# Two graph attention layers: row scores with turned probabilities replaced by transposed scores in column chunks

## The chip, the cores and the metric

The kernel runs on one core of one Trainium2 chip. The metric is the device time in microseconds (us) of one execution. The kernel before takes 551.01 us (median of 3 runs, 550.63 to 551.37).

## The reference

Four graph layers on `x` (1354 x 256, f32) with one adjacency matrix `adj` (1354 x 1354, f32, sparse, with a weighted diagonal), each followed by a residual addition and a layer norm. The change touches only the fourth, which is two attention layers in a row. Cut to what matters:

```python
def _gat_layer(x, W, adj):                # W: 256 x 512
    proj = x @ W
    Wh, Ws = jnp.split(proj, 2, axis=-1)
    scores = Wh @ Ws.T                    # 1354 x 1354
    a = jax.nn.softmax(scores, axis=-1) * adj
    out = a @ Wh
    out = out + x
    return jax.nn.leaky_relu(out, 0.01)
# L3: x = inputs; for l in range(2): x = _gat_layer(x, W_stack[l], adj)
x = _layernorm(x + _L3_gnn_ref(x, adj, L3_gnn_W_stack), axis=-1)
```

## The kernel before

The 1354 rows are T = 11 tiles of P = 128 rows (the last has 74); the 256 features are KD = 2 blocks of 128. The 1354 columns are three chunks `CH` of 512, 512 and 330, one PSUM bank of 512 f32 each. `adjT` holds the whole transposed adjacency in SBUF, `x_all` the features by rows. Each engine has one hand-written instruction stream, in the order of its block (`block.sync`, `gpsimd`, `scalar`, `vector`, `tensor`); streams meet at semaphores only. So an instruction that waits holds up everything that stands behind it on its engine.

The first three layers and their norms end with a loop over tiles in which TensorE makes the third layer's output (`c_proj`), turns the normed rows (`turn_mean`), and makes `Wh` of the first attention layer (`wh_mean`). The score matrix is computed as x (Wh-weights Ws-weights^T) x^T, with the 256 x 256 product `M3` made once.

Each attention layer then goes over the 11 row tiles, through `pipeline`, which repeats stages with fixed lags:

- TensorE: `q` (x of this tile times `M3`, 4 matmuls of 128 columns), `turn_probs` (11 transposes of 128 x 128 of the tile before), the scores of a whole row tile (`scores.__call__`, 6 matmuls into banks 0 to 2), and `agg_d` (11 matmuls of 256 columns into bank 6). In the first layer also `turn_x` and `proj_d` for the next layer's features.
- VectorE: `row_max` (one reduction over 1354 columns in PSUM), `turn_evac` (turned probabilities times `adjT`, 1408 columns from PSUM), and the finish of a tile (`gat_out`, `finish_d1` or `finish_d2`, `norm_apply_d`).
- ScalarE: `q_evac`, and `exp_row`, one exponential over 1354 columns straight from PSUM with the row's maximum as bias, which gives the row's sum as well.
- GpSimd: `store_x` in the first layer, `rsqrt_d` in the second: one small instruction a tile.

The lines that the argument names: L1278 scores, L1311 turned probabilities, L1325 sum over neighbours, L1254 q, L1240 `proj_d`, L1203 `wh_mean`, L915 row maximum, L908 and L905 evacuation with the product, L648 exponential. From an earlier stage, as prices: L771 and L773 (VectorE on two SBUF inputs of 1354 columns), L412 (GpSimd addition of 1354 columns), L838 (VectorE on PSUM and SBUF).

## Time and profile before

| | |
|---|---|
| median of 3 runs | 551.01 us (550.63 to 551.37) |
| the profiled execution's own time | 551.62 us |
| its span, first to last instruction | 549.8 us |
| TensorE busy | 503.4 us (92%), mean granted clock 0.984 |
| VectorE, ScalarE, GpSimd busy | 308.0, 197.2, 101.2 us |
| attention layers, first `q` to last sum on TensorE | 271.9 to 542.6 us |

The page gives for each engine its busy time, then 40 equal slices of the span with busy tenths, then the chain of work that ended last. The lines of an instruction group give its count, its busy time and the mean length of one. The timeline gives single instructions with start, length, and the idle time in front with what ended it.

### The profile page before, as it was taken

Reading aid. Unit: us, or ns where it says so; the run is one execution under the profiler, and the core shown is the slowest. Engines: PE = TensorE matmul, PEld = TensorE weight load, DVE = VectorE, ACT = ScalarE, POOL = GpSimd, SP = SyncE. Lnnn points to the kernel's source line nnn. Section 1 sums busy time; section 2 is a strip of 40 time slices with the busy share of each in tenths; the row PEclk is TensorE's granted clock in tenths of the full one; section 3 lists DMA queues with packets and bytes.
Section 4 is the critical chain, followed back from the end, with each engine's and each line's share of the span. In section 5 each row is a group of like instructions: output and inputs, shape, how many; then the busy total and the mean of one; then the engine's idle time right before and its main releaser. Section 6 shows DMA issues by size and latency. Waiting matters only on the chain.

```text
span 549.8 us, 6538 instructions
## 1 busy us (share of the span) xinstructions
PE 503.4 (92%) x2321; PEld 369.7 (67%) x2321; DVE 308.0 (56%) x632; ACT 197.2 (36%) x341; POOL 101.2 (18%) x120
## 2 busy tenths in 40 slices
PE   2689999999999779799889999999998999999994
PEld 1579955555555567678557777777785777767773
DVE  2489978945999758756233333333323354455544
ACT  3347729983785522243312222222222112111120
POOL 5002152602235235633000000000000000000000
PEclk9999999999999869999999999999999999999998
DMA  8445420000652000000000000000000000000000
GB/s 252 172 146 160 119 103 0 0 0 1 196 168 72 0 0 1 0 1 1 1 0 1 0 1 0 0 0 0 0 1 1 0 17 12 10 10 10 19 10 15
DMA packets 8109, 20.60 MB, mean 37 GB/s; under 512 B 944, under 2 KB 4676, under 8 KB 8088
## 3 DMA queue, kind: packets, MB, share of 16 engines
q1 hardware_dynamic: 6808, 18.75, 10.5%
q0 software_dynamic: 464, 0.79, 0.6%
q10 hardware_dynamic: 816, 0.79, 0.4%
q8 instruction: 12, 0.20, 0.2%
q14 instruction: 9, 0.07, 0.0%
HBM read 18.94 MB, written 1.39 MB: 37 GB/s over the span
## 4 chain that ended last, share of the span: by engine, by line
PE 54%; issue 26%; DVE 13%; DMA 3%; POOL 2%; ACT 2%; SPq 0%; POOLq 0%; DVEq 0%; ACTq 0%
PE psum L1325 10%; PE psum L1278 9%; PE psum L1049 9%; PE psum L1025 4%; PE psum L1136 4%; DVE eb L771 4%; DMA x_all<-in_x_dram 3%; PE psum L1311 2%; PE psum L1254 2%; PE psum L1203 2%; PE psum L981 2%; PE psum L1162 2%; PE psum L1074 2%; PE psum L1240 1%; DVE maskT L787 1%
## 5 line engine op out<-in xcount | busy, mean ns | idle before, releaser
L1325 PE MATMUL psum<-feats,probsT 128*128 128x256 f32 (+1 forms) x484 | 108.2, 379 | 0.9 <-DVE probsT L905 0.9
L1278 PE MATMUL psum<-xT,Qs 128*128 128x512 f32 (+1 forms) x264 | 104.1, 543 | 1.2 <-ACT xTs L612 0.7
L1325 PEld LDWEIGHTS psum<-feats,probsT 128*128 128x128 f32 (+1 forms) x484 | 91.6, 190 | 15.3 <-issue 1.1
L908 DVE TENSOR_TENSOR probsT<-psum,adjT 128x1408 f32<-128x1408 f32 x20 | 32.5, 1625 | 102.4 <-PE psum L1311 102.4
L1278 PEld LDWEIGHTS psum<-xT,Qs 128*128 128x128 f32 x264 | 48.4, 190 | 46.7 <-issue 41.1
L648 ACT ACTIVATE probs<-psum,negmax 128x1354 f32<-128x1354 f32 x22 | 30.6, 1390 | 101.0 <-DVE negmax L915 101.0
L915 DVE TENSOR_REDUCE negmax<-psum 128x1 f32<-128x1354 f32 x22 | 34.4, 1565 | 40.0 <-PE psum L1278 40.0
L1074 PE MATMUL psum<-eb,x_all 128*128 128x512 f32 (+3 forms) x132 | 51.4, 543 | 0.9 <-ACT eb L501 0.9
L1049 PE MATMUL psum<-adjT,x_all 128*128 128x512 f32 (+3 forms) x132 | 50.4, 542 | 0.0
L412 POOL TENSOR_TENSOR esumb<-esumb,eb 128x1354 f32<-128x1354 f32 (+1 forms) x10 | 34.8, 3476 | 58.6 <-ACT eb L501 58.6
L1074 PEld LDWEIGHTS psum<-eb,x_all 128*128 128x128 f32 (+1 forms) x132 | 25.0, 190 | 25.6 <-issue 21.1
L396 POOL TENSOR_TENSOR rstd<-veps,nhalf 128x1 f32<-128x1 f32 (+1 forms) x33 | 22.4, 678 | 104.2 <-DVE veps L716 104.2
L1049 PEld LDWEIGHTS psum<-adjT,x_all 128*128 128x128 f32 (+1 forms) x132 | 24.9, 190 | 24.6 <-issue 21.1
L1136 PE MATMUL psum<-maskT,xhl 128*128 128x512 f32 (+3 forms) x132 | 32.3, 398 | 8.8 <-POOL xhl L418 8.8
L1136 PEld LDWEIGHTS psum<-maskT,xhl 128*128 128x128 f32 (+1 forms) x132 | 25.1, 201 | 15.7 <-POOL xhl L418 11.1
L1311 PE MATMUL psum<-ident,probs 128*128 128x128 f32 x242 | 30.1, 273 | 3.0 <-issue 2.4
L438 POOL COPY x<-xs 128x256 f32 (+1 forms) x11 | 4.4, 402 | 145.6 <-DVE xs L933 145.6
L771 DVE SCALAR_TENSOR_TENSOR eb<-nslb,nsr,eb 128x1354 f32<-128x1354 f32 (+1 forms) x11 | 28.7, 2610 | 4.1 <-ACT nslb L511 3.8
L1025 PE MATMUL psum<-xw,hi 128*128 128x256 f32 (+3 forms) x121 | 30.2, 289 | 0.2 <-DVE lo L681 0.2
L486 ACT ACTIVATE signs<-signs 128x1354 bf16<-128x1354 bf16 (+1 forms) x22 | 29.3, 1333 | 0.7
L1311 PEld LDWEIGHTS psum<-ident,probs 128*128 128x128 f32 x242 | 27.1, 141 | 3.6 <-issue 2.6
L1025 PE MATMUL psum<-xw,lo 128*128 128x256 f32 (+3 forms) x121 | 29.4, 282 | 0.0
(149 smaller groups left out, 701.3 us busy)
## 6 DMA issues: line engine op xcount, KB each, us to landing
adj_rows<-in_adj_dram SPq DMA_DIRECT2D x10, 677.0 KB, 4.1
rows<-in_adj_dram SPq DMA_DIRECT2D x10, 677.0 KB, 4.0
x_all<-in_x_dram SPq DMA_DIRECT2D x1, 1280.0 KB
...
```

The source lines that it names most:

```text
L412: nc.gpsimd.tensor_tensor(esumb[0:r, 0:N], esumb[0:r, 0:N], eb[0:r, j % RING, 0:N], ALU.add)\
L648: nc.scalar.activation(probs[:, p, 0:N], psum[:, 0:len(CH), :].rearrange("p b n -> p (b n)")[:, 0:N], ACT.Exp, bias=negmax[:, p, :], accum ...
L771: own.link(nc.vector.scalar_tensor_tensor(out=e, in0=nslb[0:r, 0:N], scalar=nsr[0:r, j:j + 1], in1=e, op0=ALU.add, op1=ALU.add))
L908: nc.vector.tensor_tensor(probsT[:, p, :, :], psum[:, 3:3 + BANKS_T, :].rearrange("p b (k n) -> p (b k) n", n=P)[:, 0:T, :], adjT[:, :, ba ...
L915: nc.vector.tensor_reduce(negmax[:, p, :], psum[:, 0:len(CH), :].rearrange("p b n -> p (b n)")[:, 0:N], AX.X, ALU.max, negate=True).then_i ...
L1025: last = nc.tensor.matmul(psum[0:r, 6 + i % 2, 0:D], part[0:kk(k), i % PARTS, k, 0:r], xw[0:kk(k), k, :], start=(k == 0 and part is hi), s ...
L1049: last = nc.tensor.matmul(bank(c * KD + m, 0, c1 - c0), x_all[0:r, j, m * P:(m + 1) * P], adjT[0:r, j, c0:c1], start=(j == 0), stop=(j == ...
L1074: last = nc.tensor.matmul(bank(c * KD + m, 0, c1 - c0), x_all[0:r, j, m * P:(m + 1) * P], eb[0:r, j % RING, c0:c1], start=(j == 0), stop=( ...
L1136: last = nc.tensor.matmul(bank(c * KD + m, 0, c1 - c0), xhl[0:r, j, part, m * P:(m + 1) * P], maskT[0:r, j % MASKS, c0:c1], start=(j == 0 ...
L1278: last = nc.tensor.matmul(bank(b, 0, c1 - c0), Qs[:, p, k, :], xT[self.l][:, k, c0:c1], start=(k == 0), stop=(k == KD - 1))
L1311: last = nc.tensor.transpose(bank(3 + k // EB, (k % EB) * P, (k % EB) * P + P), probs[:, p, k * P:(k + 1) * P], ident[:, :])
L1325: last = nc.tensor.matmul(bank(6, 0, D), probsT[0:kk(k), p, k, :], wh[0:kk(k), k, :], start=(k == 0), stop=(k == T - 1))
```

## The change

Both attention layers no longer go over row tiles. They go over the three column chunks of the transposed scores: chunk numbers g = 0, 1, 2 are the first layer's, 3, 4, 5 the second's. For a chunk (here w columns wide, which are w rows of the output):

- `q_mul(g)` makes the chunk's queries transposed (`QT`), `s_tile(g, j)` the scores of all 11 source tiles j against it (2 matmuls of w columns each, banks 0 and 1 in turn).
- ScalarE's `st_copy(g, j)` brings each tile to SBUF (`ST`); VectorE's `run_max(g, j)` keeps a running maximum over the tiles. `max_turn` turns it (one transpose for 128 columns), `max_reduce` reduces it, `max_diag` makes diagonals of the negative maxima, and `max_spread` spreads them over all partitions into bank 7.
- VectorE's `soft_step(g, j)` adds them to tile j, ScalarE's `exp_probs` takes the exponential in place, GpSimd's `add_probs` adds the tile to the running sum `es` (so 10 additions and one copy a chunk), and `soft_step(g, j + 2)` multiplies tile j by `adjT`, once `add_probs(g, j)` is done.
- First layer: `sum_t(g, j)` gives the output transposed (2 matmuls of w columns for each tile), `den_t` the sums, `finish_t` divides, adds and takes the leaky relu, straight into `xT[1]`. So the 22 transposes of the second layer's x are not needed for its scores; they come back as `turn_x1`, with `x1_copy` on ScalarE, for the residual. `wh1` makes the second layer's `Wh` between the layers.
- Second layer: `sum_n(i)` gives the output by rows as before (11 matmuls of 256 columns a tile), `den_n` the row sums, `finish_n` and `finish_out` the finish.

`turn_mean(0)` also waits for `M3` now, and the loops are unrolled. The diff, cut to its core:

```diff
+            def add_probs(g, j):
+                r, w = kk(j), chunk(g)[2]
+                e = es[:, g % 2, 0:w]
+                pool.wait_ge(prob_ready.sem, g * T + j + 1)
...
+                    pool.wait_ge(es_added.sem, g * T + j)
+                    nc.gpsimd.tensor_tensor(es[0:r, g % 2, 0:w], es[0:r, g % 2, 0:w], buf(g)[0:r, j, 0:w], ALU.add)\
+                        .then_inc(es_added.sem, 1)
...
+            for i in range(4):
+                wh1_evac(i)
+            max_diag(3)
+            for i in range(4, T):
+                wh1_evac(i)
+            for j in range(7):
+                exp_probs(3, j)
+            q_evac(4)
+            for j in range(7, T):
+                st_copy(4, j - 7)
+                exp_probs(3, j)
...
+                exp_probs(4, j)
+                if j == 4:
+                    x1_copy(0)
+                    x1_copy(1)
+                if j == 8:
+                    x1_copy(2)
...
+            def run_max(g, j):
+                r, w = kk(j), chunk(g)[2]
+                m = rm[0:r, g % 2, 0:w]
...
+                elif j < T - 1:
+                    own.link(nc.vector.tensor_tensor(m, m, buf(g)[0:r, j, 0:w], ALU.max))
...
+            def soft_step(g, j):
+                c0, c1, w = chunk(g)
+                if j < T:
+                    r = kk(j)
+                    if j == 0:
+                        dve.wait_ge(max_ready.sem, g + 1)
+                    nc.vector.tensor_tensor(buf(g)[0:r, j, 0:w], buf(g)[0:r, j, 0:w], psum[0:r, 7, 0:w], ALU.add).then_inc(sub_done.sem, 1)
+                if j >= 2:
+                    r = kk(j - 2)
+                    dve.wait_ge(es_added.sem, g * T + j - 1)
+                    nc.vector.tensor_tensor(buf(g)[0:r, j - 2, 0:w], buf(g)[0:r, j - 2, 0:w], adjT[0:r, j - 2, c0:c1], ALU.mult)\
+                        .then_inc(pt_ready.sem, 1)
+            def finish_t(g):
+                c0, c1, w = chunk(g)
+                t = vbuf[:, :, :].rearrange("p (k a) n -> p k (a n)", k=KD)[:, :, 0:w]
+                dve.wait_ge(gat_den.sem, g + 1)
+                own.link(nc.vector.reciprocal(rdb[:, 0:w], bank(5, 0, w)))
+                n = own.mark(nc.vector.tensor_tensor(t, psum[:, 2:4, 0:w], rdb[:, 0:w].unsqueeze(1).to_broadcast([P, KD, w]), ALU.mult))
+                dve.wait_ge(dve_own.sem, n)
+                dve.sem_inc(gat_read.sem, 1)
+                own.link(nc.vector.tensor_tensor(t, t, xT[0][:, :, c0:c1], ALU.add))
+                nc.vector.scalar_tensor_tensor(out=xT[1][:, :, c0:c1], in0=t, scalar=SLOPE, in1=t, op0=ALU.mult, op1=ALU.max)\
+                    .then_inc(xT1_ready.sem, 1)
...
+            for j in range(T + 2):
+                soft_step(0, j)
+                if j + 5 < T:
+                    run_max(1, j + 5)
+            max_reduce(1)
+            for j in range(T + 2):
+                soft_step(1, j)
+                if j == 2:
+                    finish_t(0)
+                if j >= 3:
+                    run_max(2, j - 3)
...
+            def s_tile(g, j):
+                l, r, n = g // NC, kk(j), g * T + j
...
+                if n >= 2:
+                    pe.wait_ge(st_ready.sem, n - 1)
+                for k in range(KD):
+                    last = nc.tensor.matmul(psum[0:r, n % 2, 0:w], xT[l][:, k, j * P:j * P + r], QT[:, k, c0:c1],
+                                            start=(k == 0), stop=(k == KD - 1))
+                last.then_inc(s_done.sem, 1)
...
+            def sum_t(g, j):
+                r, w = kk(j), chunk(g)[2]
+                pe.wait_ge(pt_ready.sem, g * T + j + 1)
...
+                for m in range(KD):
+                    last = nc.tensor.matmul(bank(2 + m, 0, w), Wh[0][0:r, j, m * P:(m + 1) * P], buf(g)[0:r, j, 0:w],
+                                            start=(j == 0), stop=(j == T - 1))
...
+            def turn_x1(i):
+                r = kk(i)
+                pe.wait_ge(qT_ready.sem, KD * G)
+                if i >= 1:
+                    pe.wait_ge(x1n_ready.sem, i)
+                for k in range(KD):
+                    last = nc.tensor.transpose(psum[0:r, 4, k * P:(k + 1) * P], xT[1][:, k, i * P:i * P + r], ident[:, :])
+                last.then_inc(x1_turned.sem, 1)
...
+            for j in range(T):
+                sum_t(0, j)
+                if j == 5:
+                    max_turn(1)
+                if j == 8:
+                    max_spread(1)
+            den_t(0)
+            for j in range(T):
+                s_tile(2, j)
+            q_mul(3)
+            for j in range(T):
+                sum_t(1, j)
+                if j == 3:
+                    max_turn(2)
+                if j == 5:
+                    max_spread(2)
+            den_t(1)
+            for j in range(4):
+                s_tile(3, j)
+            for j in range(T):
+                sum_t(2, j)
+            den_t(2)
...
+            turn_x1(0)
+            turn_x1(1)
+            for g in range(NC, G):
+                den_n(g)
+                for i in tiles(g):
+                    sum_n(i)
+                    if i + 2 < T:
+                        turn_x1(i + 2)
+                    if i == 1:
+                        max_turn(5)
+                    if i == 2:
+                        max_spread(5)
```

How the instructions stand on VectorE, where one attention tile is worked on. Before, one tile of the second layer (`probs` are one row tile's probabilities; `vbuf`, `mv`, `veps`, `xs` belong to the finish of a tile):

```order
L915 TENSOR_REDUCE negmax<-psum 128x1 [waits g2_scores_done]
L908 ISA [waits g2_turned]
L908 TENSOR_TENSOR probsT<-psum,adjT 128x1408
L922 RECIPROCAL rden<-esum 128x1 [waits gat2_agg_done]
L48 ISA
L923 ISA [waits gat2_fin_chain]
L923 SCALAR_TENSOR_TENSOR vbuf<-psum,rden,x_81 128x256
```

Now, in the second layer's first chunk (ST_88 is that chunk's `ST`, ST_87 the next chunk's; L911 is the addition and L915 the product of `soft_step`, L888 is `run_max`):

```order
L915 TENSOR_TENSOR ST_88<-ST_88,adjT 128x512 [waits es_added]
L886 TENSOR_TENSOR rm<-ST_87 128x512 [waits max_turned,st_ready]
L911 TENSOR_TENSOR ST_88<-ST_88,psum 128x512 [waits dve_own]
L915 TENSOR_TENSOR ST_88<-ST_88,adjT 128x512 [waits es_added]
L888 TENSOR_TENSOR rm<-rm,ST_87 128x512 [waits st_ready]
```

Two long passes over PSUM a tile have become three of 512 columns a source tile and chunk, of which two read both inputs from SBUF and one waits for GpSimd.

ScalarE between the layers. Before (L648 is the exponential, L631 `q_evac`, L609, L612 and L619 the next layer's features):

```order
L609 ACTIVATE xT_78<-psum 128x2x128 [waits gat1_xs_turned]
L612 ACTIVATE xTs<-psum 128x256 [waits gat1_proj_done]
L619 ACTIVATE feats<-psum 128x256 [waits gat1_proj_done]
L648 ACTIVATE probs,esum<-psum,negmax 128x1354 [waits g2_turned,g2_max_ready]
```

Now (L575 `wh1_evac`, L565 `max_diag(3)`, L570 `exp_probs(3, j)`, L550 `q_evac(4)`, L557 `st_copy(4, 0)`):

```order
L575 ACTIVATE Wh_83<-psum 128x256 [waits wh1_done] x6
L575 ACTIVATE Wh_83<-psum 74x256 [waits wh1_done]
L570 ACTIVATE ST_88<-ST_88 128x512 [waits sub_done] x7
L550 ACTIVATE QT<-psum 128x512 [waits q_done] x2
L557 ACTIVATE ST_87<-psum 128x512 [waits sum_done,s_done]
```

The evacuation of chunk 4's queries, on which the 11 `s_tile(4, j)` of TensorE wait, stands behind seven exponentials of chunk 3. Further on, the copies that `turn_x1` waits for stand behind exponentials of chunk 4 (L570) in the same way (L582 is `x1_copy`):

```order
L570 ACTIVATE ST_87<-ST_87 128x512 [waits sub_done] x2
L582 ACTIVATE x1n<-psum 128x256 [waits x1_turned] x2
L570 ACTIVATE ST_87<-ST_87 128x512 [waits sub_done] x4
L582 ACTIVATE x1n<-psum 128x256 [waits gat_read,x1_turned]
```

TensorE has `turn_x1(1)`, which waits for the first of these copies, ahead of all sums of the second layer.

## Rows read from the trace of the kernel before

**Rows 1.** The page: busy time by engine; the chain that ended last.
```profile
PE 503.4 (92%) x2321; PEld 369.7 (67%) x2321; DVE 308.0 (56%) x632; ACT 197.2 (36%) x341; POOL 101.2 (18%) x120
PE 54%; issue 26%; DVE 13%; DMA 3%; POOL 2%; ACT 2%; SPq 0%; POOLq 0%; DVEq 0%; ACTq 0%
```
**Rows 2.** Chain, one tile of the first attention layer: start us, us, what.
```profile
316.10 0.89 PE psum L1254 x8
316.99 1.20 PE psum L1311 x11
318.19 0.22 PE psum L1231 x2
318.41 4.54 PE psum L1278 x12
322.95 0.86 PE psum L1240 x4
323.81 4.75 PE psum L1325 x22
```
**Rows 3.** TensorE timeline where `q` will start, and `q` now; VectorE's end.
```profile
262.76 1.03 PE L1203 MATMUL psum<-W,xT 128*128 128x256 f32 x4
263.62 0.38 PE L1194 MATMUL psum<-ident,x_all 128*128 128x128 f32 x2
271.92 1.05 PE L1254 MATMUL psum<-xT,M 128*128 128x128 f32 x8
...
542.65 0.17 DVE L922 RECIPROCAL rden<-esum 128x1 f32<-128x1 f32 x1 [1.30 <-PE psum L1325]
```
**Rows 4.** Groups by form: line, engine, out<-in, count, busy us, mean ns.
```profile
L681 DVE TENSOR_TENSOR lo<-adjT,hi 128x512 fp32r<-128x512 f32 x22 | 15.2, 692 | 2.4 <-ACT hi L467 2.4
L905 DVE TENSOR_TENSOR probsT<-psum,adjT 128x512 f32<-128x512 f32 x4 | 2.6, 686 | 1.0 <-PE psum L1311 1.0
L521 ACT ACTIVATE zT<-psum 128x512 f32<-128x512 f32 x4 | 2.4, 597 | 2.4 <-PE psum L1049 2.4
L501 ACT ACTIVATE eb<-eb 128x1354 f32<-128x1354 f32 x10 | 13.3, 1329 | 16.9 <-DVE eb L773 16.9
L543 ACT ACTIVATE vbuf<-vbuf 128x256 f32<-128x256 f32 x10 | 4.1, 407 | 6.2 <-DVE vbuf L838 6.2
L1111 PE MATMUL psum<-ones,esumb 128*128 128x1 f32 x20 | 2.3, 246 | 0.0
```
**Rows 5.** VectorE timeline, alone and then beside GpSimd.
```profile
138.14 1.63 DVE L771 SCALAR_TENSOR_TENSOR eb<-nslb,nsr,eb 128x1354 f32<-128x1354 f32 x1
142.98 4.33 DVE L771 SCALAR_TENSOR_TENSOR eb<-nslb,nsr,eb 128x1354 f32<-128x1354 f32 x1
213.15 0.47 DVE L838 SCALAR_TENSOR_TENSOR vbuf<-psum,coef,xb 128x256 f32<-128x256 f32 x1
```
**Rows 6.** GpSimd timeline at the same places.
```profile
142.82 3.06 POOL L412 TENSOR_TENSOR esumb<-esumb,eb 128x1354 f32<-128x1354 f32 x1 [5.44 <-ACT eb L501]
172.97 4.30 POOL L412 TENSOR_TENSOR esumb<-esumb,eb 128x1354 f32<-128x1354 f32 x1 [4.47 <-ACT eb L501]
213.04 0.78 POOL L424 TENSOR_TENSOR bias<-bias,x_all 128x256 f32<-128x256 f32 x1
```
**Rows 7.** Groups by form: reciprocals of 10 columns and of 1.
```profile
L828 DVE RECIPROCAL dent<-dent 128x10 f32<-128x10 f32 x1 | 0.2, 216 | 0.0
L829 DVE RECIPROCAL dent<-dent 74x1 f32<-74x1 f32 x1 | 0.2, 158 | 0.0
```
**Rows 8.** Stretches: busy time (count) of PE, PEld, DVE, ACT, POOL; granted clock.
```profile
196.00:198.00 2.00, 0.00 (x0) 0.00 (x0) 1.22 (x7) 0.88 (x3) 0.60 (x2) 0.99 0.00 0
198.00:200.00 2.00, 1.31 (x3) 1.11 (x4) 1.97 (x4) 1.13 (x3) 1.38 (x2) 0.50 0.00 0
202.00:204.00 2.00, 2.00 (x8) 1.81 (x7) 0.39 (x1) 0.00 (x0) 0.54 (x1) 0.50 0.00 0
276.00:282.00 6.00, 3.60 (x19) 2.49 (x18) 1.57 (x1) 1.75 (x3) 0.00 (x0) 1.00 0.00 0
```

More of the change, by code:

```diff
@@ new lines, in _ @@
+            for j in range(3, T):
+                while n < T and n < 2 + (j - 3) * 3 // 2:
+                    st_copy(2, n)
+                    n += 1
+                exp_probs(1, j)
+            q_evac(3)
+            max_diag(2)
+            for j in range(T):
+                exp_probs(2, j)
+            for j in range(T):
+                st_copy(3, j)
+            for i in range(4):
[3 more added lines that the diff above has]
+                wh1_evac(i)
@@ L658, in _ @@
+            x1_copy(3)
+            max_diag(5)
+            for j in range(T):
+                exp_probs(5, j)
+                if j == 4:
+                    x1_copy(4)
+                if j == 7:
+                    x1_copy(5)
+            for i in range(6, T):
+                x1_copy(i)
         @block.vector
@@ new lines, in _ @@
+            max_reduce(4)
+            for j in range(4, 7):
+                run_max(5, j)
+            for j in range(T + 2):
+                if j + 7 < T:
+                    run_max(5, j + 7)
+                soft_step(4, j)
+                if j == 6:
+                    finish_n(0)
+                if j == 7:
+                    finish_out(0)
+                if j == 9:
+                    finish_n(1)
+                if j == 10:
+                    finish_out(1)
+            max_reduce(5)
@@ L961, in _ @@
+            for j in range(T + 2):
+                soft_step(5, j)
+                if j in LATE:
+                    finish_n(LATE[j])
+                if j - 1 in LATE:
+                    finish_out(LATE[j - 1])
+            for i in range(2 + len(LATE), T):
+                finish_n(i)
+                finish_out(i)
         @block.tensor
         def _(pe):
[L963 to L966 removed]
@@ L1344, in _ @@
-            pipeline(pe, T, [(s2.q, 0), (turn_probs(G[1]), 1), (s2, 0), (agg_d(D2, G[1], Wh[1]), 1)])
+                if s == 6:
+                    q_mul(0)
+                if s >= 7:
+                    s_tile(0, s - 7)
+            for j in range(T - 6, T):
+                s_tile(0, j)
+            q_mul(1)
+            q_mul(2)
+            for j in range(T):
+                s_tile(1, j)
+                if j == 2:
+                    max_turn(0)
+                if j == 4:
+                    max_spread(0)
```

673 lines of the change are left out of this document (334 added, 339 removed).

## The prediction

> **What bounds the kernel now.** The page first: TensorE is busy 92% of the span, VectorE 56%, GpSimd 18%, and the chain that ended last is mostly TensorE [rows 1]. Then the chain in order of time, in the attention layers: one tile after the other with no gap between TensorE's pieces [rows 2]. A tile of the first layer takes 0.89 + 1.20 + 0.22 + 4.54 + 0.86 + 4.75 = 12.5 us. The two layers last from 271.9 to 542.6 us [rows 3], 270.7 us, in which TensorE waits for little. Its pieces give its prices: scores 4.54 us for 2 x 1354 = 2708 columns, sums 4.75 us for 11 x 256 = 2816, both 1.68 ns a column; a transpose is 1.20 / 11 = 0.11 us [rows 2].
>
> **TensorE's work after.** A layer has 4 x 1354 columns of q (9.1 us) and 2 x 11 x 1354 columns of scores (50.0), as before; for both layers 118.2. `sum_t` 50.0, `sum_n` 11 x 4.75 = 52.3, 22 spreading matmuls of 128 columns 4.6, `den_t` 2.3, `den_n` 11 x 0.22 = 2.4 (L1111: 2.3 us busy for 20 records, which are 10 matmuls) [rows 4], `wh1` 11 x 0.86 = 9.5, 22 + 22 transposes 4.8. Sum 244.1 us. The 242 transposes of the probabilities (22 x 1.20 = 26.4) are what goes. `q_mul(0)` can start when `wh_mean(5)` is through, at 263.6 us [rows 3]; `turn_mean(0)`'s new wait for `M3` moves that to about 264.2. Of the loop before, 5 `wh_mean` and 4 `turn_mean` remain, 5.2. If TensorE never waited, its last sum would end at 264.2 + 5.2 + 244.1 = 513.5, 29 us earlier than now. All depends on how long it waits.
>
> **What the other engines need for one source tile of 512 columns.** VectorE: addition 0.69 (PSUM and SBUF in, like L905), product 0.69 (both from SBUF, like L681), maximum 0.69 and some 0.04 for its link [rows 4]. ScalarE: copy 0.60, exponential 0.62 (between 0.407 for 256 and 1.329 for 1354 columns) [rows 4]. GpSimd: an addition of 1354 columns takes 3.06, one of 256 takes 0.78 with a wait or 0.73 [rows 6]; the line between gives 1.27 us for 512 and 0.89 for 330. Each is under or near TensorE's 1.72 us a tile, but they don't add up so simply. VectorE's L771, two inputs in SBUF, takes 1.63 us alone, and 4.33 when it starts 0.16 us after a GpSimd addition of 3.06 [rows 5, 6]: it waits the addition out and then runs. GpSimd's addition at 172.97 takes 4.30 for the same reason, the other way round [rows 6]. L838, with one input in PSUM, takes 0.47 inside a GpSimd operation, unhindered [rows 5, 6]. So products, maxima and GpSimd's additions exclude one another; the addition of the maximum does not. A `soft_step` with a maximum therefore costs 1.27 + 0.7 + 0.7 = 2.7, one alone 1.27 + 0.6 = 1.9, one of 330 columns 1.4, with a maximum of 330 beside 512 columns 2.6. The chain inside one step (addition, exponential, copy behind it on ScalarE, maximum) is 0.69 + 0.62 + 0.60 + 0.73 = 2.6 plus hand-overs, so steps with all four come to about 3.0. The Trainium skill states this as a lock, SBUF — State Buffer, section "SBUF: two separate sides": GpSimd and a VectorE operation with two SBUF inputs hold the shared port pair for the whole instruction, and the other one fully blocks. It speaks against this change. By that rule, the trace agrees: steps cost 2.7 and 1.9; without it they would cost 2.1 and 1.4.
>
> **Where TensorE waits**, walked through in program order with these numbers, each instruction starting when its engine and its releasers are done. The marks of the walk, on TensorE: chunk 0's scores end at 291.7 us (264.2 + 3.4 for q + 5 turns of the mixed loop at 2.8 + 6 x 1.72), the two next q at 297.4, `s_tile(1, 4)` at 306.4 with `run_max(1, 4)` behind it at 308.4, `den_t(0)` 345, `max_spread(2)` 382, `den_t(2)` 414, `s_tile(3, 10)` 426, `wh1` 438, `s_tile(4, 10)` 472, `s_tile(5, 10)` 489.
>
> - `max_spread(1)` needs `max_reduce(1)`, which stands behind all 13 steps of `soft_step(0)` on VectorE. These start at 308.4 and take 2 x 2.7 + 4 x 3.1 + 6 x 1.9 = 29 us to about 338; diagonals 1.4 more. TensorE, at `sum_t(0, 8)`, is through at 337.5 and waits 2.4.
> - `finish_t(0)` stands between the steps of chunk 1 and starts when `den_t(0)` ends, 345. It is a reciprocal of 512 columns (bounds 0.7 us, the price of any operation, and 3.4, from the slope of 58 ns for 9 columns [rows 7]; I take 3.0, since these rows are reciprocals), a product of 1024 columns 1.2 and two passes 2.5. ScalarE's `exp_probs(1, 3)` waits for it, behind that `st_copy(2, 2)`, behind that `s_tile(2, 4)`: 1.2 + 4.4 us of waiting, then 2.3 more as copies come at VectorE's pace.
> - `max_turn(2)` comes when the steps of chunk 1, 2.6 each, are over: 3.1.
> - `s_tile(3, 2)` needs `st_copy(3, 0)`, which stands behind all exponentials of chunk 2: 3.0.
> - `wh1` and `max_diag(3)` share ScalarE, whose order holds `wh1_evac(4)` back: 1.2.
> - `s_tile(4, 0)` needs `q_evac(4)` behind `exp_probs(3, 6)`. The exponentials start after `wh1_evac(10)` at 438.6, GpSimd's sum paces the seven (four products at 1.9), so QT is there at 449.4; TensorE was ready at 442.1: 7.3.
> - `turn_x1(1)` needs `x1_copy(0)` behind `exp_probs(4, 4)`. Scores end at 489.4, VectorE begins `soft_step(4, 0)` at 486.3 and reaches the fifth addition at 496, copy at 497.2: 7.8.
> - The rest: two evacuations before chunk 5's scores 1.6, `turn_x1(3)` behind `exp_probs(4, 8)` 1.2, `max_spread(5)` behind the 13 steps of chunk 4 and two `finish_n` of 2.3 each 3.6, `den_n(4)` behind `finish_n(3)` and `turn_x1(5)` behind `exp_probs(5, 4)` 4.0, `den_n(5)` and the last two of these 1.9.
>
> Sum 2.4 + 7.9 + 3.1 + 3.0 + 1.2 + 7.3 + 7.8 + 1.6 + 1.2 + 3.6 + 4.0 + 1.9 = 45.0 us.
>
 Of the waits above, seven are 3 us or more; before most of them other engines set the pace afterwards anyway, so I count the two longest: 6.4 us. Bounds: 0, and 22 for all seven.
>
> **The sum.** 264.2 + 5.2 + 244.1 + 45.0 + 6.4 = 564.9 for the last sum, 7.2 behind it for the last tile's finish and its store as now (549.8 less 542.6), and 1.8 for what lies around the span (551.62 less 549.8): 573.9 us, which I give as 574. The sum is made against the profiled execution, 551.62, which is 0.6 us above the median, less than it can be trusted to. A fifth of a per cent, 1.1 us, is about what a measurement can tell from no change.
>
> **Rivals.**
>
> - *TensorE stays the bound, and the change is faster.* The hand-over orders between VectorE and GpSimd could be kinder than walked: where GpSimd's additions fall beside the additions of the maximum, steps cost 2.1 and 1.4, and the reciprocal 0.7. Then the waits that only order imposes remain: 1.2 + 1.7 at chunk 2, 4.4 and 5.5 at the two long ones, some 5 at the rest, 18 us, no half clock: 513.5 + 18 + 7.2 + 1.8 = 540.5. For it: VectorE is at 56% and has room. Against: rows 5 and 6 show whole blocking, and additions of the maximum are a third of VectorE's passes. It decides below some 29 us of waits and lost clock together. Chance 0.22.
> - *The exclusion bites half of the time*: half of the difference, about 557. Chance 0.06.
> - *The clock falls after every long wait*: five more times 3.2 us, 590. For it: all seven are about as long as 196 to 198 with what lies round it. Against: the pace there is set elsewhere. Chance 0.12.
> - *The change doesn't do what it says*: transposed scores could cost more columns, if the last tile of 74 rows or the chunk of 330 were padded. The instruction order shows them cut to size; I give it nothing.
>
> **How the numbers follow.** The forecast has 0.60, with a range of its own from 562 to 586 (reciprocal at either bound, two clock drops more or none). For 8 in 10 the range must reach into the first rival: 543 to 590. Faster by over 0.2%: 0.22 and 0.02 of the forecast's lower edge, 0.24. Within 0.2%: 0.03. Slower: 0.73.
>
> **What would show it.** TensorE busy falls by some 18 us in these layers while its idle time rises to 40 or 50 us, over a dozen gaps; the longest released by ScalarE's QT and x1n. VectorE's products and maxima at 512 columns show a mean well over 0.69 us, near 1.2, and GpSimd's additions over 1.27. GpSimd's busy time rises by 65 us or more (40 additions of 1.27, 20 of 0.89, the copies, less today's small operations). The granted clock has slices at 5 to 8 in the last third. I would be wrong if products and GpSimd additions overlap at their lone lengths, or if QT for chunk 4 is there within 2 us of TensorE's wish.

## The result and the profile after

The changed kernel takes 582.67 us (median of 4 runs, 580.23 to 585.03); the kernel before took 551.19 us beside it (4 runs, 550.63 to 554.15). The ratio is 1.0567, with an interval of 1.0514 to 1.0620: slower, by 31.5 us. The profiled execution took 582.08 us, its span is 580.3.

The page of the changed kernel: busy time by engine, the granted clock in 40 slices, and the chain by engine, beside [rows 1].

```profile
PE 502.2 (87%) x1935; PEld 327.9 (57%) x1935; DVE 384.4 (66%) x754; ACT 236.6 (41%) x430; POOL 181.5 (31%) x175
...
PEclk9989999999999799999999997998999899597998
...
PE 56%; DVE 24%; POOL 7%; ACT 6%; issue 4%; DMA 2%; SPq 0%; POOLq 0%; DVEq 0%; ACTq 0%
```

TensorE has 386 instructions fewer and is busy as long as before (502.2 against 503.4 us). VectorE has 76 us more, GpSimd 80. The chain has moved from TensorE's issue to VectorE and GpSimd. In the last third the clock has slices at 5, 7 and 8.

TensorE's timeline, the pieces at the marks and before the longer waits (the bracket is the wait in front of a piece and what ended it; L1299 is `s_tile`, L1335 `sum_t`, L1283 `q_mul`, L1322 `max_spread`, L1377 `turn_x1`, L1391 `sum_n`):

```profile
263.66 3.60 PE L1283 MATMUL psum<-xT,M 128*128 128x512 f32 x8
...
291.14 5.82 PE L1283 MATMUL psum<-xT,M 128*128 128x512 f32 x16
...
339.44 1.27 PE L1322 MATMUL psum<-dg,ones 128*128 128x128 f32 x8 [2.17 <-ACT dg L565]
...
354.04 9.18 PE L1299 MATMUL psum<-QT,xT 128*128 128x330 f32 x24 [4.58 <-ACT ST L557]
...
399.35 14.14 PE L1335 MATMUL psum<-ST,Wh 128*128 128x330 f32 x44 [3.29 <-DVEq L926]
...
425.90 3.62 PE L1357 MATMUL psum<-W,xT 128*128 128x256 f32 x16
...
448.03 22.36 PE L1299 MATMUL psum<-QT,xT 128*128 128x512 f32 x44 [5.98 <-ACT QT L550]
...
497.36 0.66 PE L1377 MATMUL psum<-ident,xT 128*128 128x128 f32 x2 [8.07 <-ACT x1n L582]
...
499.38 7.98 PE L1391 MATMUL psum<-Wh,ST 128*128 128x256 f32 x22
...
507.42 4.92 PE L1391 MATMUL psum<-Wh,ST 128*128 128x256 f32 x22
...
522.70 1.53 PE L1322 MATMUL psum<-dg,ones 128*128 128x128 f32 x6 [3.22 <-ACT dg L565]
...
563.60 9.67 PE L1391 MATMUL psum<-Wh,ST 128*128 128x256 f32 x44
```

The marks of the walk hold for 225 us: chunk 0's scores end at 291.1 (walk 291.7), `wh1` starts at 425.9 (426), `s_tile(4, 10)` ends at 470.2 (472), `s_tile(5, 10)` at 488.9 (489). One is off: `max_spread(2)` starts at 378.9 instead of 382. The two long waits are where they were put, 5.98 us behind QT (7.3) and 8.07 behind x1n (7.8). The last sum ends at 573.3 instead of 564.9, and behind the mark at 489 the miss shows openly. That the marks before it hold so well is luck in part: up to there TensorE waited 22.9 us, 7.6 less than in the walk, and a slower clock and longer work filled the difference. The rows at 499.38 and 507.42 show the clock: the same work, one `sum_n` of 11 matmuls (22 records in the trace), takes 7.98 us behind the wait and 4.92 us eight microseconds later.

Stretches of the changed kernel, columns as in [rows 8]:

```profile
448.00:452.00 4.00, 3.97 (x5) 1.85 (x6) 2.18 (x4) 0.15 (x1) 2.44 (x2) 0.50 0.01 2
452.00:456.00 4.00, 4.00 (x8) 1.55 (x7) 0.54 (x1) 2.08 (x4) 1.26 (x1) 0.72 0.00 0
...
500.00:504.00 4.00, 4.00 (x11) 3.19 (x10) 1.45 (x3) 0.63 (x1) 2.35 (x2) 0.50 0.00 0
504.00:508.00 4.00, 4.00 (x17) 3.36 (x17) 0.48 (x1) 0.00 (x0) 0.00 (x0) 0.82 0.00 0
508.00:512.00 4.00, 4.00 (x21) 3.46 (x19) 3.83 (x11) 0.70 (x2) 1.44 (x2) 1.00 0.00 0
```

TensorE works without a gap from 500 to 508, with a granted clock of 0.50 (1.2 GHz) and then 0.82. No wait lies inside these pieces, so no other engine sets their pace, and VectorE in its turn waits for the sum (its first `finish_n`, at 507.50, stands idle for 6.05 us behind it). What a higher clock gives back there is measured in e5.

What three engines need for a source tile (groups of the changed kernel by form; count, busy us, mean ns):

```profile
L384 POOL TENSOR_TENSOR es<-es,ST 128x512 f32<-128x512 f32 x36 | 53.6, 1488 | 38.9 <-ACT ST L570 36.7
...
L915 DVE TENSOR_TENSOR ST<-ST,adjT 128x512 f32<-128x512 f32 x40 | 35.6, 890 | 8.0 <-POOL es L384 4.5 <-POOL es L381 3.4
L911 DVE TENSOR_TENSOR ST<-ST,psum 128x512 f32<-128x512 f32 x40 | 26.9, 681 | 6.2 <-PE psum L1322 5.6
L888 DVE TENSOR_TENSOR rm<-rm,ST 128x512 f32<-128x512 f32 x32 | 25.9, 811 | 23.2 <-ACT ST L557 23.0
...
L923 DVE RECIPROCAL rdb<-psum 128x512 f32<-128x512 f32 x2 | 6.7, 3352 | 1.5 <-PE psum L1346 1.5
```

The same at single instructions, VectorE first, then GpSimd:

```profile
456.19 0.69 DVE L911 TENSOR_TENSOR ST<-ST,psum 128x512 f32<-128x512 f32 x1
456.79 1.05 DVE L915 TENSOR_TENSOR ST<-ST,adjT 128x512 f32<-128x512 f32 x1
457.76 1.80 DVE L888 TENSOR_TENSOR rm<-rm,ST 128x512 f32<-128x512 f32 x1
```
```profile
456.02 1.27 POOL L384 TENSOR_TENSOR es<-es,ST 128x512 f32<-128x512 f32 x1 [1.72 <-ACT ST L570]
457.74 1.28 POOL L384 TENSOR_TENSOR es<-es,ST 128x512 f32<-128x512 f32 x1 [0.45 <-ACT ST L570]
```

The addition (one input in PSUM) runs at 0.69 us inside GpSimd's addition. The product starts at 456.79, inside GpSimd's addition that ends at 457.29, and ends at 457.84; the maximum starts 0.02 us behind GpSimd's next addition, which ends at 459.02, and ends at 459.56. Both come out 0.55 us after GpSimd. It is the exclusion of [rows 5, 6], at 512 columns.

### The profile page after: what moved, and what is told of

It reads as the page before. It is cut to its first block, busy times and chain, and to the rows that moved or that the text cites. A ratio compares the mean times of both kernels' runs of the same rounds, so it can differ in the third digit from the quotient of the medians.

```text
span 580.3 us, 5714 instructions
## 1 busy us (share of the span) xinstructions
PE 502.2 (87%) x1935; PEld 327.9 (57%) x1935; DVE 384.4 (66%) x754; ACT 236.6 (41%) x430; POOL 181.5 (31%) x175
## 4 chain that ended last, share of the span: by engine, by line
PE 56%; DVE 24%; POOL 7%; ACT 6%; issue 4%; DMA 2%; SPq 0%; POOLq 0%; DVEq 0%; ACTq 0%
PE psum L1299 12%; PE psum L1107 9%; PE psum L1391 7%; PE psum L1335 5%; POOL es L384 4%; PE psum L1083 4%; DVE eb L773 4%; DVE ST L911 3%; PE psum L1194 3%; PE psum L1283 3%; DMA x_all<-in_x_dram 2%; DVE rm L888 2%; PE psum L1039 2%; ACT ST L570 2%; DVE ST L915 2%
## 5 line engine op out<-in xcount | busy, mean ns | idle before, releaser
L1299 PE MATMUL psum<-QT,xT 128*128 128x512 f32 (+3 forms) x264 | 109.6, 567 | 16.0 <-ACT ST L557 9.4
L384 POOL TENSOR_TENSOR es<-es,ST 128x512 f32<-128x512 f32 (+3 forms) x60 | 80.0, 1333 | 45.4 <-ACT ST L570 41.4
L1299 PEld LDWEIGHTS psum<-QT,xT 128*128 128x128 f32 (+1 forms) x264 | 50.3, 195 | 68.9 <-issue 54.6
L570 ACT ACTIVATE ST<-ST 128x512 f32<-128x512 f32 (+3 forms) x66 | 37.6, 579 | 87.6 <-DVE ST L911 87.6
L557 ACT ACTIVATE ST<-psum 128x512 f32<-128x512 f32 (+3 forms) x66 | 35.5, 541 | 70.8 <-PE psum L1299 70.8
L915 DVE TENSOR_TENSOR ST<-ST,adjT 128x512 f32<-128x512 f32 (+3 forms) x66 | 51.3, 781 | 14.2 <-POOL es L384 10.2
L1391 PE MATMUL psum<-Wh,ST 128*128 128x256 f32 (+3 forms) x242 | 60.4, 411 | 0.0
L888 DVE TENSOR_TENSOR rm<-rm,ST 128x512 f32<-128x512 f32 (+1 forms) x48 | 38.1, 795 | 30.8 <-ACT ST L557 30.5
L1335 PE MATMUL psum<-ST,Wh 128*128 128x512 f32 (+3 forms) x132 | 53.5, 559 | 3.6 <-DVEq L926 3.3
L1391 PEld LDWEIGHTS psum<-Wh,ST 128*128 128x128 f32 (+3 forms) x242 | 48.8, 205 | 8.4
L911 DVE TENSOR_TENSOR ST<-ST,psum 128x512 f32<-128x512 f32 (+3 forms) x66 | 40.1, 618 | 11.8 <-PE psum L1322 11.2
L1335 PEld LDWEIGHTS psum<-ST,Wh 128*128 128x128 f32 (+1 forms) x132 | 25.4, 196 | 28.7 <-issue 23.3
L773 DVE SCALAR_TENSOR_TENSOR eb<-nslb,nsr,eb 128x1354 f32<-128x1354 f32 (+1 forms) x11 | 28.7, 2611 | 4.1 <-ACT nslb L463 3.8
```

The source lines that it names most:

```text
L384: nc.gpsimd.tensor_tensor(es[0:r, g % 2, 0:w], es[0:r, g % 2, 0:w], buf(g)[0:r, j, 0:w], ALU.add)\
L570: nc.scalar.activation(buf(g)[0:r, j, 0:w], buf(g)[0:r, j, 0:w], ACT.Exp).then_inc(prob_ready.sem, 1)
L773: own.link(nc.vector.scalar_tensor_tensor(out=e, in0=nslb[0:r, 0:N], scalar=nsr[0:r, j:j + 1], in1=e, op0=ALU.add, op1=ALU.add))
L888: own.link(nc.vector.tensor_tensor(m, m, buf(g)[0:r, j, 0:w], ALU.max))
L911: nc.vector.tensor_tensor(buf(g)[0:r, j, 0:w], buf(g)[0:r, j, 0:w], psum[0:r, 7, 0:w], ALU.add).then_inc(sub_done.sem, 1)
L915: nc.vector.tensor_tensor(buf(g)[0:r, j - 2, 0:w], buf(g)[0:r, j - 2, 0:w], adjT[0:r, j - 2, c0:c1], ALU.mult)\
```

## The experiments

Each kernel was timed against the kernel before, which took 551.1 to 551.6 us in the four sessions. "Work" below is TensorE's time from the start of `q_mul(0)` to the end of the last sum, less its waits (summed over its timeline) and less added fillers; the sum of the prediction has 249.3 us for it at full clock.

**e1 and e2: what GpSimd's additions cost, and how.** e1 makes them one column wide; e2 puts three fills of the full width in their place, each behind the one before. Neither makes the sum of the exponentials.

```diff
-                    nc.gpsimd.tensor_tensor(es[0:r, g % 2, 0:w], es[0:r, g % 2, 0:w], buf(g)[0:r, j, 0:w], ALU.add)\
+                    nc.gpsimd.tensor_tensor(es[0:r, g % 2, 0:1], es[0:r, g % 2, 0:1], buf(g)[0:r, j, 0:1], ALU.add)\
```
```diff
-                    nc.gpsimd.tensor_tensor(es[0:r, g % 2, 0:w], es[0:r, g % 2, 0:w], buf(g)[0:r, j, 0:w], ALU.add)\
+                    nc.gpsimd.memset(es[:, g % 2, 0:w], 1.0).then_inc(pool_own.sem, 1)
+                    pool.wait_ge(pool_own.sem, owned[0])
+                    nc.gpsimd.memset(es[:, g % 2, 0:w], 1.0).then_inc(pool_own.sem, 1)
+                    pool.wait_ge(pool_own.sem, owned[0])
+                    nc.gpsimd.memset(es[:, g % 2, 0:w], 1.0).then_inc(es_added.sem, 1)
```

> Leaves out the sum of the exponentials: GpSimd's 60 additions work on one column instead of 512 or 330, and its six copies become fills with 1.0, at the same places in the order. Exclusion theory (GpSimd's additions and VectorE's operations with two SBUF inputs block one another): the means of the 512-column product and maximum fall from 0.89 and 0.81 us to 0.69 to 0.72, steps without a maximum from 1.9 to about 1.3 us, steps with one stay near 2.7 to 2.8 (their chain addition, exponential, copy, maximum is 2.7). TensorE's wait before the first layer's second spread (2.2 us) and before the third chunk's sums (3.3) go, the wait for chunk 4's queries falls from 6.0 to about 3, that for the first x1n copy from 8.1 to about 6; with less time at the half clock the run is 15 to 25 us faster, 558 to 568 us. Rival (VectorE's long operations are long for another reason, memory traffic or operand kinds): their means stay, and only GpSimd's latency goes; 575 to 582 us.

> Leaves out the sum of the exponentials too: each GpSimd addition is replaced by three linked fills of the same columns with 1.0, which take GpSimd about as long (I expect 1.2 to 1.5 us in all for 512 columns) but read nothing from SBUF. Exclusion theory, in the form that GpSimd must read SBUF to block an operation with two SBUF inputs: the product's and maximum's means are 0.69 to 0.72 as in the kernel with tiny additions, while the pace of the steps without a maximum is GpSimd's, 1.3 to 1.6 us; 562 to 574 us. Rival (GpSimd's pace alone is what costs, blocking adds nothing): time within 3 us of the changed kernel, 580 to 585. If writes alone block as well: means stay at 0.8 to 0.9.

e1: 557.7 us (557.0 to 558.2), ratio 1.0132 (1.0091 to 1.0173). e2: 568.81 us (567.5 to 569.35), ratio 1.0325 (1.0282 to 1.0369). Groups of e1 (product, maximum), then of e2 (product, maximum, one of the fills):

```profile
L915 DVE TENSOR_TENSOR ST<-ST,adjT 128x512 f32<-128x512 f32 x40 | 27.4, 684 | 3.4 <-POOL es L381 3.1 <-POOL es L384 0.2
...
L888 DVE TENSOR_TENSOR rm<-rm,ST 128x512 f32<-128x512 f32 x32 | 22.1, 691 | 25.4 <-ACT ST L557 25.2
```
```profile
L922 DVE TENSOR_TENSOR ST<-ST,adjT 128x512 f32<-128x512 f32 x40 | 27.5, 688 | 10.5 <-POOL es L392 7.2 <-POOL es L383 3.1
...
L895 DVE TENSOR_TENSOR rm<-rm,ST 128x512 f32<-128x512 f32 x32 | 22.1, 691 | 25.3 <-ACT ST L564 24.9
L389 POOL MEMSET es<- 128x512 f32 x40 | 21.0, 525 | 2.3
```

Fills don't hold VectorE up: products are at 688 ns although GpSimd is at work at least as long as before (85.9 us of fills, 80.0 of additions). So of the 25.0 us between the change and e1, 11.1 are GpSimd's pace (e2 less e1), and 13.9 the exclusion (the change less e2), each with the clock that its waits cost. Three fills with their hand-overs take some 1.7 us (525 ns each and 0.06 us between them), longer than one addition of 1.27 us, so 13.9 is a lower bound. And e1, nearly free of both (its additions still take 0.34 us), is still slower than the kernel before: what is left eats all that TensorE saves. e1 lies 0.3 us under the range that was expected for the exclusion, e2 inside it.

**e3, e4 and e6: the two long waits, one each and together.** e3 puts `q_evac(4)` behind four exponentials of chunk 3 instead of seven. e4 has `turn_x1(0)` and `turn_x1(1)` among the scores of chunk 5 and their copies earlier. e6 has both.

```diff
-            for j in range(7):
+            for j in range(4):
                 exp_probs(3, j)
             q_evac(4)
```
```diff
+            x1_copy(0)
...
-                if j == 4:
-                    x1_copy(0)
+                if j == 1:
                     x1_copy(1)
...
+                    turn_x1(0)
+                if j == 9:
+                    turn_x1(1)
```

> Only ScalarE's order between the layers: chunk 4's queries are evacuated behind the fourth exponential of chunk 3 instead of behind the seventh, and the copies of chunk 4's scores stand between the later exponentials. Order theory: TensorE's 6.0 us wait for QT falls to under 1 us and the following stretch at the half clock (3.3 us lost) goes; the time won holds until VectorE, whose steps of chunk 3 and maxima of chunk 4 then end behind TensorE, takes part of it back: 5 to 9 us faster than the changed kernel, 574 to 578 us. Rival (VectorE and GpSimd set the end of the layer whatever the order): the wait only moves to the next meeting point, the fourth maximum, and the time stays within 2 us.

> Only the residual's turns: turn_x1(0) and turn_x1(1) stand among chunk 5's scores on TensorE and their copies before and behind the second exponential of chunk 4 on ScalarE. Order theory: the wait of 8.1 us before the second layer's first sums goes and with it the half clock there (3 to 4 us lost), so sums of tiles 0 and 1 are done 10 us earlier. But the third sum waits for finish_n(0), which stands on VectorE behind seven steps of chunk 4, and max_spread(5) behind all thirteen: so most of it is given back there, and the run is 2 to 5 us faster, 578 to 581. Rival (TensorE's wait is the bound there): 9 to 12 us faster, 570 to 574.

> Both moves of order together: q_evac(4) behind four exponentials instead of seven, and the first two turns of x and their copies ahead of chunk 4's exponentials. Alone they gave 8.8 and 4.8 us. If the waits are independent, the sum, 13.6 us: 569. If what one saves is lost at the next wait (VectorE's and GpSimd's work of chunk 3 and 4 must be done anyway before den_n and max_spread(5)), less: 572 to 576. PE idle from 263 us on: 38.9 less 6 and 3, about 29 to 31.

e3: 573.88 us (572.06 to 575.23), ratio 1.0424 (1.0375 to 1.0473). e4: 577.83 us (576.2 to 578.85), ratio 1.0485 (1.0438 to 1.0532). e6: 570.62 us (568.64 to 572.04), ratio 1.0347 (1.0308 to 1.0385). They gave 8.8, 4.8 and together 12.1 us of the 13.6, so the two waits are mostly independent. e3 and e4 lie 0.1 and 0.2 us under the ranges of the order theory and e6 between its two cases. TensorE's timeline in e3 and in e4:

```profile
444.32 15.72 PE L1299 MATMUL psum<-QT,xT 128*128 128x512 f32 x36 [0.69 <-ACT QT L550]
...
490.93 0.66 PE L1377 MATMUL psum<-ident,xT 128*128 128x128 f32 x2 [8.07 <-ACT x1n L582]
```
```profile
451.15 22.34 PE L1299 MATMUL psum<-QT,xT 128*128 128x512 f32 x44 [6.00 <-ACT QT L550]
...
510.62 0.66 PE L1377 MATMUL psum<-ident,xT 128*128 128x128 f32 x2 [7.62 <-ACT x1n L582]
```

In e3 the first wait is gone, with the slow scores behind it (nine tiles at 1.75 us; all eleven had taken 22.36), and the second is unchanged. In e4 the wait for x1n hasn't gone but moved, behind the second sum: `turn_x1(3)` needs `x1_copy(2)`, which stands behind `exp_probs(4, 8)`. Moving one instruction shows the next one that is late.

**e5: the clock alone.** TensorE gets 244 transposes of the identity, 27.8 us of work, just ahead of the instructions that wait.

```diff
+            def fill(count, b):
+                for n in range(count):
+                    nc.tensor.transpose(bank(b, (n % 4) * P, (n % 4 + 1) * P), ident[:, :], ident[:, :])
...
+            fill(52, 2)
             for j in range(T):
                 s_tile(4, j)
```

> Only TensorE gets more to do: transposes of the identity (0.11 us each at the full clock) before the instructions that wait longest: 70 before turn_x1(1), 52 before s_tile(4, 0), 40 before s_tile(2, 4), 28 before sum_t(2, 0), 28 before max_spread(5), 17 before turn_x1(5), 9 before den_n(4). Theory A (the clock term was mis-sized; each of these waits is followed by some 8 to 12 us at half clock, about 16 us in all, of which the path carries most): the stretches behind the waits stay at a granted clock near 1.0, and the time falls by 8 to 16 us although work is added: 567 to 575. Theory B (VectorE and GpSimd set the pace behind the waits anyway, as the prediction assumed for all but two of them): the fillers gain at most the 6 us of the two longest, 576 to 583, and TensorE's waits grow by what its work shrinks. Slower than the change would mean that fillers hold TensorE past the moment it is released.

570.92 us (569.74 to 572.45), ratio 1.0348 (1.0321 to 1.0375): 11.8 us faster than the change, by adding work. TensorE's timeline, the scores of chunk 4 and the first sum by rows, then two stretches of e5:

```profile
449.03 19.30 PE L1299 MATMUL psum<-QT,xT 128*128 128x512 f32 x44 [0.35 <-ACT QT L550]
...
496.38 5.00 PE L1391 MATMUL psum<-Wh,ST 128*128 128x256 f32 x22
```
```profile
448.00:452.00 4.00, 3.65 (x14) 1.88 (x13) 2.87 (x5) 1.93 (x5) 3.42 (x2) 1.00 0.00 0
...
500.00:504.00 4.00, 4.00 (x21) 3.51 (x20) 2.30 (x8) 0.00 (x0) 0.58 (x2) 1.00 0.00 0
```

QT comes within 1 us of where it came in the change; the scores behind it take 19.30 instead of 22.36 us, the sum 5.00 instead of 7.98. From the start of `q_mul(0)` to the end of the last sum e5 takes 297.3 us, the change 309.6: 12.3 us less, so theory A holds. At one place theory B does. The change has six tiles of chunk 2's scores in 9.18 us at 354.04, at half clock; e5 has the same six at full clock, but with waits for copies between them:

```profile
356.70 3.65 PE L1299 MATMUL psum<-QT,xT 128*128 128x330 f32 x12 [0.22 <-ACT ST L557]
361.47 1.35 PE L1299 MATMUL psum<-QT,xT 128*128 128x330 f32 x4 [1.12 <-ACT ST L557]
363.21 2.46 PE L1299 MATMUL psum<-QT,xT 128*128 128x330 f32 x8 [0.39 <-ACT ST L557]
```

They end at 365.67, 8.97 us after they start, and `q_mul(3)` starts 20.87 us after `den_t(0)` in both kernels. There ScalarE's copies set the pace, and the slow clock cost nothing.

**e7: other orders at every wait.** The same instructions: `max_reduce(1)` two steps earlier; copies of chunks 2, 3, 4 and 5 between the exponentials of the chunk before; `finish_t(1)` among chunk 2's steps; `wh1` (in one bank) and `s_tile(3, 4)` to `(3, 7)` among the sums of chunk 2; the first x turns ahead of chunk 4's exponentials; four `finish_n` among chunk 4's steps. Two of the places:

```diff
-                while n < T and n < 2 + (j - 3) * 3 // 2:
+                while n < T and n < 7 + (j - 3) * 3 // 2:
                     st_copy(2, n)
...
-            finish_t(1)
-            for j in range(4):
-                run_max(3, j)
+                if j == 3:
+                    finish_t(1)
+                if 4 <= j <= 11:
+                    run_max(3, j - 4)
```

> The same instructions as the change in other orders, at all waits of the walk: max_reduce(1) two steps earlier, finish_t(1) among the steps of chunk 2, copies of chunk 3 and 4 between the exponentials of the chunk before, wh1 and four s_tile(3, j) among the sums of chunk 2, the first x turns ahead of chunk 4's exponentials, four finish_n among chunk 4's steps, max_reduce(5) at its eleventh step. Theory A (what costs the change its gain is mostly the position of instructions in fixed streams, the work itself would fit beside TensorE's 244 us): PE idle from 263 us on falls from 38.9 to 12 to 22 us, the clock loss from 21 to 8 to 12, and the time to 540 to 555. Theory B (VectorE with GpSimd's lock is the bound from chunk 1 on: 66 soft steps of 2.6 to 3 us with finishes are about 200 us and more): idle only moves to other places, 562 to 575.

561.91 us (558.4 to 563.15), ratio 1.0171 (1.0133 to 1.021): 20.8 us better than the change, but theory A asked for at least 27.7; the time lies at the edge of theory B's 562 to 575. Waits sum to 28.7 us, not to 12 to 22. TensorE's timeline shows the two that the new order made, behind `finish_t(2)` and behind chunk 4's steps with the four finishes among them:

```profile
420.28 7.11 PE L1301 MATMUL psum<-QT,xT 128*128 128x512 f32 x12 [5.07 <-DVE xT L936]
...
507.50 0.90 PE L1313 MATMUL psum<-ident,rm 128*128 128x128 f32 x3 [9.29 <-DVE rm L898]
```

**e8: those two places.** `den_t(2)` ahead of most of `wh1` and `s_tile(3, j)`; `q_mul(4)` between `max_turn(3)` and `max_spread(3)`; sums by rows in banks 0 to 3 in turn; two of the four finishes behind `max_reduce(5)`; `max_turn(5)` inside `sum_n(4)`.

```diff
             den_t(2)
+            s_tile(3, 6)
+            s_tile(3, 7)
+            for i in range(4, 8):
+                wh1(i)
...
-                b = 2 + i % 2
+                b = (i + 2) % 4
```

> The reordered version with its three remaining losses attacked: all sums of chunk 2 and den_t(2) come before most of wh1 and s_tile(3, j), so that finish_t(2) runs behind them (was a wait of 5.1 us); q_mul(4) fills the time between max_turn(3) and max_spread(3); and the sums by rows use banks 0 to 3 in turn, with max_turn(5) inside the first sum of chunk 4 and two of the four finish_n behind max_reduce(5) (was a wait of 9.3 us). Theory A (position in the streams is what is left): the layer boundary gives 7 to 9 us, the last one 3 to 6 with its half clock, 545 to 552, at or just under the kernel before. Theory B (VectorE with the lock is the bound of the second layer, 13 steps of 2.6 to 2.9 us a chunk and 2.9 us for each finish_n beside them): what is gained at the layer boundary is lost again at the end, 556 to 562.

560.15 us (559.58 to 564.32), ratio 1.0185 (1.0147 to 1.0224). The number is theory B's; the trace shows waits that order made. The scores of chunk 5 end 7 us earlier than in e7, and then (TensorE's timeline, L1379 is `den_n`):

```profile
498.58 1.87 PE L1379 MATMUL psum<-ones,es 128*128 128x1 f32 x8 [10.94 <-POOL es L384]
...
533.08 1.27 PE L1379 MATMUL psum<-ones,es 128*128 128x1 f32 x6 [6.93 <-POOL es L384]
```

`den_n(4)` and `den_n(5)` stand ahead of their chunk's sums and wait for the whole running sum; the sums behind them need single products only, and `max_turn(5)` stood in one of these sums.

**e9: one more move of order.** `den_n(4)` and `den_n(5)` behind the first sum of their chunk, and `wh1` in banks 4 and 6 in turn.

```diff
-            for g in range(NC, G):
-                den_n(g)
-                for i in tiles(g):
-                    if i >= 2:
-                        turn_x1(i)
-                    sum_n(i)
-                    if i == 4:
-                        max_spread(5)
+            for i in range(T):
+                if i >= 2:
+                    turn_x1(i)
+                sum_n(i)
+                if i == 4:
+                    max_spread(5)
+                if i % 4 == 0:
+                    den_n(NC + i // 4)
```

> e8 with two places mended. den_n(4) and den_n(5) stand behind the first sum of their chunk instead of ahead of it: there they waited 10.9 and 6.9 us for GpSimd's whole running sum, and the sums that need only single products, and max_turn(5), waited with them. And wh1 uses banks 4 and 6 in turn instead of bank 4 alone (seven waits of 0.56 us). Theory A (position): soft_step(5, 0) starts 7 to 9 us earlier, wh1 gives 4 us, both on the path: 547 to 552, level with the kernel before. Theory B (VectorE with the lock bounds the second layer): the sums trickle at VectorE's pace, and only the part after the last product moves: 554 to 558.

541.47 us (539.25 to 542.89), ratio 0.982 (0.9789 to 0.9851): faster than the kernel before by 10 us and than the change by 41, and 5.5 us under theory A's lower end. Against e8 the waits are 18.0 us shorter and the work 2.3. No run separates the two moves, nor the order from the banks (`wh1` in 4 and 6, the sums by rows in 0 to 3). e9's page, the longest waits of TensorE's timeline, and the groups of product and maximum:

```profile
PE 488.9 (91%) x1935; PEld 321.8 (60%) x1935; DVE 388.7 (72%) x754; ACT 236.8 (44%) x430; POOL 180.4 (33%) x175
```
```profile
484.99 0.41 PE L1392 MATMUL psum<-ident,xT 128*128 128x128 f32 x2 [1.44 <-ACT x1n L582]
...
492.35 0.70 PE L1408 MATMUL psum<-Wh,ST 128*128 128x256 f32 x2 [2.11 <-DVE ST L927]
...
499.54 6.72 PE L1408 MATMUL psum<-Wh,ST 128*128 128x256 f32 x22
```
```profile
L927 DVE TENSOR_TENSOR ST<-ST,adjT 128x512 f32<-128x512 f32 x40 | 34.0, 851 | 6.0 <-POOL es L384 4.0 <-POOL es L381 1.9
L900 DVE TENSOR_TENSOR rm<-rm,ST 128x512 f32<-128x512 f32 x32 | 28.0, 875 | 24.2 <-ACT ST L557 24.1
```

The engines have as many instructions as in the change, VectorE and GpSimd are busy as long (388.7 against 384.4 us, 180.4 against 181.5), and the exclusion is still there (851 and 875 ns, not 690). What is gone is most of TensorE's waiting, 9.7 us instead of 38.9, and most of the half clock behind it: its work takes 257.5 us instead of 270.7, 2.9 more than in e5.

All of them side by side, the parts of TensorE's time from the profiled executions (us):

| kernel | median | start of `q_mul(0)` | waits | fillers | work | end of last sum |
|---|---|---|---|---|---|---|
| predicted | 574.0 | 264.2 | 45.0 | | 249.3 + 6.4 | 564.9 |
| the change | 582.7 | 263.7 | 38.9 | | 270.7 | 573.3 |
| e1 | 557.7 | 263.5 | 22.9 | | 261.8 | 548.2 |
| e2 | 568.8 | 264.7 | 29.8 | | 265.5 | 560.1 |
| e3 | 573.9 | 263.6 | 32.6 | | 268.2 | 564.4 |
| e4 | 577.8 | 266.8 | 36.3 | | 266.9 | 569.9 |
| e5 | 570.9 | 266.3 | 14.9 | 27.8 | 254.6 | 563.6 |
| e6 | 570.6 | 265.1 | 30.9 | | 264.8 | 560.8 |
| e7 | 561.9 | 264.2 | 28.7 | | 259.5 | 552.4 |
| e8 | 560.2 | 264.0 | 27.7 | | 259.8 | 551.5 |
| e9 | 541.5 | 264.8 | 9.7 | | 257.5 | 532.0 |

## Why the prediction was right, and where its sum was off

The prediction said slower, 574.0 within 543 to 590; measured 582.7.

- **TensorE's work.** Right within 2% at full clock. The 242 transposes are gone, and pieces in undisturbed stretches have nearly the lengths given (`s_tile(3, 4)` to `(3, 10)` 1.74 us each against 1.72, `sum_n` 4.92 against 4.75, `q_mul(0)` 3.60 against 3.4). e5, with a granted clock of 1.00 throughout, needs 254.6 us, 5.3 over the 249.3 of the sum. Counted in its timeline from each piece's start to the next one's, less the waits, they are spread thin: scores 102.3 us against 100.0, `sum_n` 53.2 against 52.3, `sum_t` 50.8 against 50.0, spreads 5.2 against 4.6, `wh1` 9.9 against 9.5, turns 5.1 against 4.8.
- **VectorE and GpSimd exclude one another.** Right in kind, as the single instructions above show: GpSimd's addition takes 1.27 us alone, as interpolated. The mean of the product is 0.89 us rather than near 1.2, for many fall between two additions; by the means alone it looks like the rival in which the exclusion bites half of the time. Where steps follow one another without a maximum they do take what the whole exclusion gives, 1.9 us each in chunk 0 (VectorE, 327.61 to 333.29). e1 and e2 give the exclusion at least 13.9 us and GpSimd's pace 11.1. The rule that was cited from the Trainium skill (SBUF — State Buffer, "SBUF: two separate sides") agrees, also in that GpSimd's fills leave VectorE alone (688 ns, e2).
- **The reciprocal.** Taken at 3.0 us, measured 3.35 for 512 columns and 2.22 for 330 in the groups, between the bounds and near the slope of [rows 7]. The estimate of 4.3 us from the repeat count of 8 in the Trainium skill (VectorE: DVE Perf Modes, "Walkthrough: the 8-slice pipeline in each mode") would have been 0.95 us too long.
- **The waits.** 38.9 us instead of 45.0. Term by term, predicted and measured: `max_spread(1)` 2.4, 2.2; chunk 2's scores behind `finish_t(0)` 7.9, 5.1; `max_turn(2)` 3.1, none; chunk 3's early copies 3.0, none; in their place `sum_t(2, 0)` waited 3.3 for `finish_t(1)` (row 399.35), which the list does not have; `wh1` 1.2, 0.7; QT 7.3, 6.0; x1n 7.8, 8.1; `max_spread(5)` 3.6, 3.2; `den_n(4)` and `turn_x1(5)` 4.0, 2.9; the rest 4.7, 3.4. So two waits of the list did not come, one came that it lacks, and the others are mostly a little shorter. The list is also shorter than its own walk: between the marks at 306.4 (`s_tile(1, 4)`) and 337.5 (`sum_t(0, 8)`) lie 27.1 us of TensorE's work at the walk's prices, so the walk waits 4.0 us there, and the sum leaves them out. With them the forecast would have been 578. Measured there: 1.3, 1.3 and 0.3 us.
- **The clock: the step that failed in size.** "before most of them other engines set the pace afterwards anyway, so I count the two longest: 6.4 us." By e5 TensorE's work is 270.7 less 254.6, 16.1 us longer for it, and 12.3 of these were on the path, twice what the sum has. The two longest were priced nearly right: behind x1n `den_n(3)` takes 1.71 instead of 0.95 us and the first sum 7.98 instead of 5.00, behind QT the scores 22.36 instead of 19.30, together 6.8 us. The other five were put at nothing. The clock fell at four more places, and against e5 the premise of the sum, that another engine sets the pace there, holds at the first: six tiles of scores 9.18 us at 354.04 instead of 6 x 1.11, which cost nothing. It fails at the next, the sums at 399.35 with 14.14 instead of 12.45. Behind `max_spread(5)` (1.53 instead of 0.94) it holds for `sum_n(3)`, 5.89 instead of 4.96, which a wait for x1n took up. It fails at the last, with `den_n(4)` 1.84 instead of 1.02 and `sum_n(4)` 7.29 instead of 5.00. The failing ones cost some 5.4 us.
- **The sum closed.** 564.9 less 0.5 for the start, less 6.1 for the waits, plus 9.7 for the clock, plus 5.3 for the rest of the work gives 573.3, where the last sum ends. It has to, since work is here what the waits leave; what it shows is that the errors have both signs, and that the waits made up for most of the clock. Behind the last sum come 8.8 us, as predicted 9.0.
- **TensorE busy.** Predicted some 18 us less, and 1.2 less on the page: at half clock the same work is more busy time.
- **The rivals.** The faster case, 540.5 us, did not come about, since its condition did not hold: the exclusion is whole. e9 comes to 541.5 by another way, with the exclusion in place and the instructions moved; that the two numbers are so close is chance. So the positions in the fixed streams, with the banks that go with them, decided: of the 41 us between the change and e9, e1 with next to no cost of GpSimd recovers 25, e9 with all of it 41. The case with half clock behind every long wait, 590, had the clock right: it fell behind every wait of 3 us or more that came. That the time stayed at 582.7 is due to shorter waits than forecast and to the place where the copies hid it.
